# Routing, first loads, last stores' waits and output stage of a one-core attention and experts kernel

## The reference

```python
xn = layernorm(x)                          # no scale, no bias
qkv = xn @ Wqkv                            # 16 heads of 16
Q, K = rope(Q), rope(K)                    # pairs (2i, 2i+1) are turned
attn = softmax(causal(Q @ K.T * 0.25)) @ V
a = attn @ Wout + bout
p = softmax(xn @ gate_w.T + gate_b)        # 10 gates: 8 experts, 2 null
weights, selected = top_k(p, 2)            # weights of true experts, normalised
f = sum over the two of w_e * (xn @ expert_w[e] + expert_b[e])
out = x + a + f
```

## Time and profile before

| | |
|---|---|
| median of 3 runs | 989.14 us (989.03 to 990.25) |
| profiled execution, its own time | 994.68 us |
| its span, first to last instruction | 993.0 us |
| mean granted clock of TensorE | 0.969 |
| TensorE busy | 902.7 us (91%) |
| DVE, ACT, POOL busy | 84%, 74%, 47% |
| moved by DMA | 106.65 MB |

### The profile page before, as it was taken

How to read it: one execution, slowest core, us unless ns; L and a number is a source line. 1 busy time by engine, 2 the same in 40 slices (tenths; PEclk the granted TensorE clock), 3 DMA queues, 4 the chain that set the end, 5 groups by cost and what they waited for, 6 DMA issues and landing times. The chain is left out here.

```text
span 993.0 us, 22231 instructions
## 1 busy us (share of the span) xinstructions
PE 902.7 (91%) x7911; PEld 395.2 (40%) x7911; DVE 837.9 (84%) x1112; ACT 737.8 (74%) x1556; POOL 463.2 (47%) x588
## 2 busy tenths in 40 slices
PE   2888457999999999999999999999999999999888
PEld 1544233232432344444443544353444333322267
DVE  5999879999899978987889788978888899894856
ACT  3566323788788888888888789878887888789822
POOL 4677748585200353344834574355142344355620
PEclk9999775999999999999999999999999999999989
DMA  9777820301200424345414542265334321122113
GB/s 323 265 257 252 281 73 22 97 3 41 68 2 2 118 81 124 87 131 149 129 55 117 151 147 69 77 170 139 66 90 126 97 59 50 34 58 67 39 53 128
DMA packets 82133, 106.65 MB, mean 107 GB/s; under 512 B 10048, under 2 KB 59112, under 8 KB 81000
## 3 DMA queue, kind: packets, MB, share of 16 engines
q1 hardware_dynamic: 74536, 85.83, 27.2%
q0 software_dynamic: 6528, 17.83, 7.3%
q10 hardware_dynamic: 960, 1.57, 0.5%
HBM read 67.37 MB, written 37.50 MB: 106 GB/s over the span
## 5 line engine op out<-in xcount | busy, mean ns | idle before, releaser
L1306 DVE TENSOR_REDUCE blk<-psP 128x2 f32<-128x1024 f32 (+2 forms) x560 | 623.1, 1159 | 91.4 <-PE psP L1466 46.6
L1239 ACT ACTIVATE probs<-psS 128x512 f32<-128x512 f32 (+3 forms) x1280 | 588.0, 540 | 101.8 <-PE psS L1521 96.0
L1521 PE MATMUL psS<-Qs,Ks 50*128 50x512 f16 (+3 forms) x1280 | 329.1, 352 | 11.5 <-ACT probs L1239 7.0
L1463 PE MATMUL psP<-Ks,Qs 48*128 48x512 f16 (+2 forms) x1264 | 294.3, 359 | 22.6 <-DVE blk L1306 9.1
L1583 PE MATMUL psO<-probs,Vs 128*32 128x512 f32 (+3 forms) x2560 | 299.3, 545 | 6.0 <-POOL probs L1139 4.9
L1139 POOL TENSOR_SCALAR_AFFINE_SELECT probs<-probs 128x512 f32<-128x512 f32 x128 | 88.3, 690 | 337.6 <-ACT probs L1239 301.3
L1521 PEld LDWEIGHTS psS<-Qs,Ks 50*128 50x128 f16 x1280 | 96.0, 93 | 240.5 <-ACT probs L1239 155.2
L1463 PEld LDWEIGHTS psP<-Ks,Qs 48*128 48x128 f16 x1264 | 79.9, 94 | 119.6 <-DVE blk L1306 77.1
L1466 PE MATMUL psP<-later,eye 64*128 64x128 bf16 x1024 | 103.7, 222 | 0.0
L1583 PEld LDWEIGHTS psO<-probs,Vs 128*32 128x32 f32 x2560 | 52.8, 108 | 85.8 <-issue 65.1
L1466 PEld LDWEIGHTS psP<-later,eye 64*128 64x128 bf16 x1024 | 78.5, 99 | 19.9 <-issue 2.2
(11 more groups left out here) (186 smaller groups left out, 770.2 us busy)
## 6 DMA issues: line engine op xcount, KB each, us to landing
xn<-we_scratch SPq DMA_DIRECT2D x72, 256.0 KB
expert_scratch<-xn SPq DMA_DIRECT2D x36, 256.0 KB, 3.4
v_scratch<-vst SPq DMA_DIRECT2D x8, 1024.0 KB, 4.0
qk_scratch<-part SPq DMA_DIRECT2D x32, 256.0 KB, 4.0
Vs<-v_scratch SPq DMA_DIRECT2D x16, 512.0 KB, 3.9
Qs<-qk_scratch SPq DMA_DIRECT2D x168, 32.0 KB
Ks<-qk_scratch SPq DMA_DIRECT2D x168, 32.0 KB
acc<-x SPq DMA_DIRECT2D x8, 512.0 KB, 9.4
```

What stands on the lines that cost most here:

```text
L1239: nc.scalar.activation(probs[u % NPR][:, h, q0:CH], psS[:, k % SB, q0:CH], ACT.Exp, scale=exp_scale).then_inc(s_read[k % SB], 1)
L1306: nc.vector.tensor_reduce(out, src, AX.X, ALU.max).then_inc(item_ok[slot], 1)
L1463: ins = pe.matmul(psP[:, slot, at:at + w], Qs[r][rows, qt // CT, p, t * P:(t + 1) * P], Ks[r][rows, kc, p, 0:w], start=True, stop=True)
L1521: pe.matmul(psS[:, k % SB, q0:CH], Ks[r][rows, kt // CT, p, kt % CT * P:(kt % CT + 1) * P], Qs[r][rows, c, p, q0:CH], start=True, stop=Tru ...
```

## The change

The last slice's `values` come before its queries 2 and 3. `low_e` of experts 6 and 7 and `split(LAST, 3)` move from DVE to POOL; ACT scales the weights in place for it. The routing has fewer and smaller steps: the first gate needs no maximum of its own, rows are summed in blocks of four tiles before TensorE counts and ranks, the prefix over experts is a product and a sum on DVE, and the expert table is made with a tile in each partition, then stored to HBM and loaded back as one row. SP issues the 12 loads of `Qs[0]` before its last q/k stores, ACT those of `Ks[0]`. SP's waits for the last q/k, expert and bias stores stand in its attention program behind the V loads. POOL raises `item_ok` first. The output stage is in the attention's block: tiles are turned in `psS`, products go to the two slots of `psP`, and the idle transposes are gone.

```diff
                 sp.wait_ge(v_ok, ONE + 2 * s + 2)
...
+                if s == LAST:
+                    for k in range(QKT):
+                        sp.wait_ge(part_stored[k], ONE + 16 * LAST)
+                    load_heads(sp, qk_s, Qs[0], 0, Q_PARTS, slice(0, CHUNKS), 0, ahead_in)
...
-                    sp.wait_ge(el_ok, ONE + e + 1)
-                    sp.dma_start(we_s[e], wep[e % 2][:, :, :, :].rearrange("p w k n -> p (w k n)")
-                                 ).then_inc(e_stored[e % 2], 16)
+                    for late in {LAST - 1: (), LAST: (LAST - 1, LAST)}.get(e, (e,)):
+                        sp.wait_ge(el_ok, ONE + late + 1)
+                        sp.dma_start(we_s[late], wep[late % 2][:, :, :, :].rearrange("p w k n -> p (w k n)")
+                                     ).then_inc(e_stored[late % 2], 16)
+            sp.wait_ge(be_ok, ONE + 1)
+            sp.dma_start(be_s.rearrange("e p d -> e (p d)"), be_p[:, :, :].rearrange("e p d -> e (p d)")).then_inc(be_stored, 16)
             for b in range(2):
                 sp.wait_ge(v_stored[b], ONE + 16 * CHUNKS)
-                sp.wait_ge(e_stored[b], ONE + 16 * EXPERTS // 2)
-            for k in range(QKT):
-                sp.wait_ge(part_stored[k], ONE + 16 * NB * CHUNKS)
-            sp.wait_ge(be_ok, ONE + 1)
-            sp.dma_start(be_s.rearrange("e p d -> e (p d)"), be_p[:, :, :].rearrange("e p d -> e (p d)")).then_inc(spare, 16)
             sp.wait_ge(ahead_in, ONE + 16 * 2 * LOADS)
-            sp.wait_ge(spare, ONE + 16 * (2 + NB * CHUNKS))
+            sp.wait_ge(spare, ONE + 16 * (1 + NB * CHUNKS))
...
                         low(s, k0)
+                        if s == LAST:
+                            if k0 == 2:
+                                low(s, 3)
+                            low_e(LAST - 1 + k0 // 2)
+            def low_e(e):
+                pool.wait_ge(eh_ok, ONE + e + 1)
+                nc.gpsimd.tensor_tensor(wep[e % 2][:, 1, :, :], we_sb[:, :, e * D:(e + 1) * D], wep[e % 2][:, 0, :, :],
+                                        ALU.subtract).then_inc(el_ok, 1)
...
+                if e >= LAST - 1:
+                    ins.then_inc(whole_ok, 1)
+                    act.wait_ge(whole_ok, ONE + e - LAST + 2)
+                    ins = nc.scalar.activation(we_sb[:, :, e * D:(e + 1) * D], we_sb[:, :, e * D:(e + 1) * D], ACT.Copy,
+                                               scale=wscale[:, OF_E:OF_E + 1])
+                ins.then_inc(eh_ok, 1)
...
             load_heads(act, qk_s, Ks[0], 1, K_PARTS, slice(0, CHUNKS), 0, ahead_in)
-            load_heads(act, qk_s, Qs[0], 0, Q_PARTS, slice(0, CHUNKS), 0, ahead_in)
...
-                    if not first:
+                    if not first and s < LAST:
                         low_e(s - 1)
...
-            low_e(LAST)
...
-            split(LAST, 3)
...
-            def largest(into, of):
-                step(nc.vector.tensor_reduce(gm[:, :], of, AX.X, ALU.max))
-                stepped()
-                step(nc.vector.tensor_tensor(into, of, wide(gm[:, :]), ALU.is_equal))
-                stepped()
-                step(nc.vector.tensor_tensor(into, into, row(lower[:, :]), ALU.mult))
-                stepped()
+            def foremost(into):
                 step(nc.vector.tensor_reduce(gr[:, :], into, AX.X, ALU.max))
                 stepped()
...
-            largest(hot[0][:, :, :], lg[:, :, :])
+            step(nc.vector.scalar_tensor_tensor(out=hot[0][:, :, :], in0=lg[:, :, :], scalar=0.0, in1=row(lower[:, :]),
+                                                op0=ALU.is_ge, op1=ALU.mult))
+            stepped()
+            foremost(hot[0][:, :, :])
...
+            step(nc.vector.tensor_reduce(gm[:, :], gq[:, :, :], AX.X, ALU.max))
+            stepped()
+            step(nc.vector.tensor_tensor(hot[1][:, :, :], gq[:, :, :], wide(gm[:, :]), ALU.is_equal))
+            stepped()
+            step(nc.vector.tensor_tensor(hot[1][:, :, :], hot[1][:, :, :], row(lower[:, :]), ALU.mult))
+            stepped()
+            foremost(hot[1][:, :, :])
...
+            dve.wait_ge(sent_ok, ONE + 1)
+            with nc.allow_low_precision(reason="counts up to 32 are whole numbers"):
+                nc.vector.tensor_reduce(some[:, :, :], sent[:, 0:TILES, :].rearrange("p (b t) e -> p b e t", t=BLOCK), AX.X,
+                                        ALU.add).then_inc(blocks_ok, 1)
+                dve.wait_ge(blocks_ok, ONE + 1)
+                nc.vector.tensor_reduce(total[:, :], some[:, :, :].rearrange("p b e -> p e b"), AX.X, ALU.add
+                                        ).then_inc(blocks_ok, 1)
+            none = (gm, gr)
+            for i in range(2):
+                step(nc.vector.tensor_tensor(none[i][:, :], hot[i][:, :, EXPERTS], hot[i][:, :, EXPERTS + 1], ALU.add))
...
             dve.wait_ge(count_ps, ONE + 1)
-            step(nc.vector.tensor_scalar_add(count[:, :], psV[0:EXPERTS, 1, 0:P], float(P - 1)))
+            step(nc.vector.tensor_scalar_add(count[:, :], psV[:, 1, 0:EXPERTS], float(P - 1)))
             stepped()
             step(nc.vector.tensor_single_scalar(count[:, :], count[:, :], 7, ALU.logical_shift_right))
             stepped()
-            nc.vector.tensor_copy(countb[:, :], count[:, :]).then_inc(count_ok, 1)
-            dve.wait_ge(first_ps, ONE + 1)
-            step(nc.vector.tensor_scalar_mul(first[:, :, :], psV[:, 2, 0:2 * EXPERTS].rearrange("p (i e) -> p i e", i=2),
-                                             float(P)))
+            step(nc.vector.tensor_copy(countf[:, :], count[:, :]))
+            stepped()
+            step(nc.vector.tensor_tensor(shares[:, :, :], upto[:, :, :, :].rearrange("p i e f -> p (i e) f"),
+                                         countf[:, :].unsqueeze(1).to_broadcast([P, 2 * EXPERTS, EXPERTS]), ALU.mult))
+            stepped()
+            step(nc.vector.tensor_reduce(first[:, :, :].rearrange("p i e -> p (i e)"), shares[:, :, :], AX.X, ALU.add))
...
+            dve.wait_ge(ahead_ps, ONE + 1)
...
-                step(nc.vector.tensor_tensor(gm[:, :], hot[i][:, :, EXPERTS], hot[i][:, :, EXPERTS + 1], ALU.add))
...
+                step(nc.vector.scalar_tensor_tensor(out=idx[:, i, :], in0=none[i][:, :], scalar=lost[:, i:i + 1],
...
-            step(nc.vector.tensor_tensor(past[:, :, :], first[:, 1, :].unsqueeze(1).to_broadcast([P, MTILES, EXPERTS]),
-                                         row0[:, :].unsqueeze(2).to_broadcast([P, MTILES, EXPERTS]), ALU.is_le))
-            stepped()
-            step(nc.vector.tensor_reduce(row0[:, :], past[:, :, :], AX.X, ALU.add))
-            stepped()
-            step(nc.vector.tensor_scalar_min(etab[:, :], row0[:, :], float(EXPERTS - 1)))
+            step(nc.vector.tensor_scalar(past[:, :], first[:, 1, :], row0[:, 0:1], None, ALU.is_le))
+            stepped()
+            step(nc.vector.tensor_reduce(number_past[:, :], past[:, :], AX.X, ALU.add))
+            stepped()
+            step(nc.vector.tensor_scalar_min(eplace[:, :], number_past[:, :], float(EXPERTS - 1)))
...
                     queries(s, b, 2)
                     queries(s, b, 3)
                     if s == 0:
                         pe.wait_ge(w_step, ONE + WE)
-                    values(s, b)
+                    if s < LAST:
+                        values(s, b)
             for j in range(CHUNKS):
...
-            width = (TILES + 1) * EXPERTS
-            for t in range(TILES):
-                ins = pe.matmul(psV[0:EXPERTS, 1, 0:P], sent[:, t, :], full[:, :], start=(t == 0), stop=(t == TILES - 1))
-            ins.then_inc(count_ps, 1)
-            pe.matmul(psV[:, 0, 0:width], upper[:, :], flat, start=True, stop=True)
-            for t in range(1, TILES + 1):
-                pe.matmul(psV[:, 0, t * EXPERTS:width], full[:, :], flat[:, 0:width - t * EXPERTS], start=False, stop=True,
-                          skip_group_check=True)
-            pe.wait_ge(count_ok, ONE + 1)
-            pe.matmul(psV[:, 2, 0:2 * EXPERTS], countb[:, :], upto[:, :, :].rearrange("p i e -> p (i e)"), start=True,
-                      stop=True).then_inc(first_ps, 1)
-def attend(nc, qk_s, v_s, we_s, be_s, xd, ys, wout, escale, idx, unscale, etab, Qs, Ks, Vs, xn, acc, hot, ge, eye, later, identf,
-           identh, wo, on, wsel, bo, second, lane, number, at):
+            width = TILES * EXPERTS
+            rank = psV[:, 0, 0:width]
+            inside = rank.rearrange("p (b n) -> p b n", b=BLOCKS)
+            blocks = flat[:, 0:width].rearrange("p (b n) -> p b n", b=BLOCKS)
+            pe.matmul(rank, upper[:, :], flat[:, 0:width], start=True, stop=True)
+            for t in range(1, BLOCK):
+                pe.matmul(inside[:, :, t * EXPERTS:BLOCK * EXPERTS], full[:, :], blocks[:, :, 0:(BLOCK - t) * EXPERTS],
+                          start=False, stop=True, skip_group_check=True)
+            pe.wait_ge(blocks_ok, ONE + 2)
```

(68 more changed lines are left out.)

122 lines of the change are left out of this document (49 added, 73 removed).

## The result

The changed kernel took 981.97 us, the median of four runs (981.49 to 983.54), against 989.11 for the kernel before beside it (989.03 to 990.25): ratio 0.9925, 95% interval 0.9913 to 0.9937, so 7.1 us faster. The forecast was 978.7, 10.4 us faster. The profiled execution is that of 983.54 us, with a span of 980.6.

A forecast was written before the change was run, and what follows sets the result against it. TensorE was 91% busy; the change touched two seams, the first held by DVE's chain, the second by a barrier before output. -1.2 - 6.72 + 1.2 + 0.17 - 1.05 - 2.8 = -10.4 us, from 989.14 to 978.7; range 975.5 to 983.

The forecast's parts named there:

- Projection's last slice: End of the projection: reordered `values` +0.3, `low_e(LAST)` leaving DVE -1.5, so -1.2 us.
- Routing: DVE's routing chain before the first barrier: fewer and smaller steps, -6.72 us.
- What that gives back: DVE's routing: POOL's added subtractions lengthen four two-input DVE instructions by 0.3 each, +1.2 us.
- rival with full blocking: First barrier: POOL's subtractions cost DVE 4.2 instead of 1.2, giving 981.7 us; a later barrier had chance 0.16.
- First loads on two queues: Before the first barrier: `Ks` on ACT, `Qs` on SP, landed by 125.8, hidden by DVE ending at 126.65; zero.
- my own sign: First barrier: the prediction is wrong if `Ks` land after DVE ends.
- `Ks` land as late as the 24 did: First barrier: `Ks` land at 128.7, moving it by 2.1, to 980.8 us; a later barrier had chance 0.16.
- Moved waits: SP's store waits moved into its attention program: stores land near the barrier, later work has time to spare; zero.
- Semaphore order: Behind the first barrier: TensorE starts at once, DVE's first reduce waits for `item_ps` instead, -1.05 us.
- Output stage: Seam from attention to output: no barrier, two `turn_out` for seven idle transposes, first product earlier, -2.8 us.
- cold rival: Output stage starts at half clock with fewer idle transposes, up to 1013 us; chance 0.07, shared with other losses.
- kinder clock: Attention's opening: TensorE's clock is up instead of at half, up to 4 us less, 975 us; chance 0.10.

The follow-up runs named there:

- f1: z1 with the three subtractions added to GpSimd in the last slice cut to 8 columns; one execution, 983.94 us.
- a1: The changed kernel with the loads of `Qs` back on ACT's queue behind `Ks`; ratio 0.9892 (0.9867 to 0.9917).
- h1: z1 with SP's waits for the last q/k, expert and bias stores put back before the barrier; 978.76 to 980.15 us.
- d1: The kernel before with only `item_ok` raised first among the 48 semaphores; ratio 0.9972 (0.9952 to 0.9992).
- c1: The kernel before with only the output stage moved into the attention's block; ratio 0.9957 (0.9937 to 0.9977).
- z1: a1 with each load halved, the halves needing only slices 0 to 3 issued by SP in slices 3 to 6; ratio 0.9902 (0.9870 to 0.9934).

## Why the prediction was right, and where it was too large

- **Projection's last slice, -1.2 with +0.17 at the start:** right. The bias addition went from 111.71 to 110.72, -0.99.
- **Routing, -6.72:** right in its main part. From `sent` to L714 are 2.89 us, 2.84 forecast; from there to the end 3.94, 3.91 forecast. Ahead of `sent` one size was wrong: the instruction that does equality and multiply (L670) took 1.25 us, also in f1, where I had L648's 0.84.
- **What that gives back, +1.2:** too small. f1 measured 2.0. I took four instructions at 0.3; L674 alone lost 0.75. The rival with full blocking (4.2) was further off, on the other side. With the 0.8 from here, the 0.4 of L670 and 0.2 of smaller steps DVE ended at 128.04, not at 126.65: 1.4 us.
- **First loads on two queues, "hidden by DVE, with 0.9 us to spare":** the step that failed, and the largest error. I let `Ks` land 3.4 us behind their issue, at 125.8, as the 24 loads had, and called issue time the limit. Issue ended at 118.6, earlier than I had it (it began at 113.9, not at 116.2: ACT's rounding doesn't wait for GpSimd's subtractions), but the last load landed at 130.3, 2.3 us behind DVE's end. By my own sign ("if `Ks` land after DVE ends") this part is wrong. a1 shows that issue was not the limit: issued 6.5 us later, the last load lands 1.2 us earlier. The transfer fits: 1.57 MB at the 156 to 194 GB/s that loads reach alone is 8 to 10 us, and the q/k stores move beside it. I had set the loads against 367 GB/s, which is a window of stores. The 3.4 us of the earlier trace rows was only the tail of the transfer. How much of the 11.7 us from last issue to landing is the loads' own and how much the stores' is open. With DVE's end moved forward by 5.3 the loads became the bound; 2.5 of the 5.3 were lost. The rival "`Ks` land as late as the 24 did" had this outcome, with 128.7 for a landing that came at 130.3. The split itself was not neutral: a1 shows one queue landing them 0.8 to 1.2 earlier.

The Trainium skill (DMA: Bandwidth & Descriptors, Why a DMA increments its semaphore by 16 and not by 1) has a DMA run on the largest number of engines, up to 16, that divides the slowest dimension of both sides. Each load here writes 8 partitions, so by that rule it gets 8 of 16 engines; the share of 0.53 at 122 to 126 us in the kernel before, with loads alone, agrees. By that rule the 24 loads take, as an estimate, twice the time that their bytes would take on 16 engines, which no issue time shows.

- **Moved waits, 0:** right only by luck. I had the last stores landed near the barrier, behind DVE's end. h1 finds 0 with one queue, where they land near 122.8. But the split, which I priced at nothing, held them back to 131.4 and 132.6, behind the loads. Left ahead of the barrier, the waits would have put it some 2.3 us later (an estimate: 132.6 less 130.3). Two terms put at nothing hid each other.
- **Semaphore order, -1.05:** right; -1.1 in d1's trace, -1.2 to -1.4 in its times. In the changed kernel itself memset to first reduce is 2.10 against 3.49, -1.4.
- **Output stage, -2.8:** right; c1 has -2.4 in the trace and -2.6 to -3.2 in the times. In the changed kernel's profile the clock stayed full from 172 to 980 us, so the cold rival fell. There was no kinder clock at the first seam either: between 96 and 196 us it is at half for 54.6 us in both profiles, and it rises for good some 39 us behind DVE's first reduce in the one as in the other.

The sum by measured sizes: DVE's end -5.3, loads +2.5, semaphores -1.4, output -2.4, so -6.6 against -7.1 timed; with the -3.2 that the output has in c1's lower group it is -7.4. Both differ from 7.1 by less than the attention's middle, from the first reduce to the last product, varies between executions (812.3 to 814.6 us in the eight with the long mask). 981.97 lies within 975.5 to 983.0, but outside the forecast's own 977 to 981, to which I gave 0.62: it lies where I had put the later barrier, with 0.16.

## What to carry to other kernels

When a chain that hides transfers gets shorter, ask when the last byte lands, not when the last load is issued: bytes over the rate of the windows in which nothing else moves, and the queueing of every store beside it. Loads put ahead of stores on one queue delay the stores too, so look for who waits for those. A seam's gain is what the next-latest of its waits allows; early halves of the loads (z1) turned the rest of the routing's gain into time. Long runs of back-to-back two-input instructions on DVE are better placed where GpSimd has nothing on the critical path; the traces argue for it, and no run here shows the gain in time.

## What the runs showed that I had not expected

- A GpSimd mask of 0.69 us took 7.2 us beside DVE's back-to-back additions, and ended 0.5 us behind the last of them: held off over some 16 successive DVE instructions. In other executions of the same program it got in (0.86), and the additions took 446 ns in place of 422. The Trainium skill (SBUF — State Buffer, Terms) has the loser of the shared port pair block for one whole instruction; here it blocked over many. What decides between the two is open. Of what it costs, some 1.9 us are the half clock behind the wait.
- GpSimd's subtractions stretched one of DVE's two-input instructions from 0.57 to 1.32 us and its neighbours by 0.2 to 0.4; one number for the contention doesn't fit.
- SP's q/k stores, issued beside the loads on its own queue, took up to 14.2 us to land, 5.4 with one queue of loads, and nothing in the time shows it, because the same change had moved the waits for them.
